# First expert layer: expert outputs scaled by their gates on leaving PSUM and summed by accumulating scatters in a chain; the tail reads one row per token

## The reference

```python
x = x + gnn0(layernorm(x))          # masked attention over a graph
x = x + ffn0(layernorm(x))          # experts, the two best of 8 for each token
x = x + gnn1(layernorm(x))          # message passing, two dense layers
x = x + ffn1(layernorm(x))          # attention, then the single best of 8 experts
```

```python
raw_weights = softmax(flat_x @ gate_w + gate_b)
top_w, top_idx = top_k(raw_weights, 2)
gate_output = (one_hot(top_idx, 8) * top_w[..., None]).sum(axis=-2)
h = gelu(einsum('td,edh->teh', flat_x, w1) + b1)
expert_out = einsum('teh,ehd->ted', h, w2) + b2
combined = einsum('ted,te->td', expert_out, gate_output)
```

## Time and profile before

| | us |
|---|---|
| median of 3 runs | 1104.51 (1102.79 to 1106.34) |
| the profiled execution | 1104.55 |
| its span, first to last instruction | 1102.8 |
| PE, DVE, ACT, POOL busy in the span | 884.4, 764.6, 506.7, 360.4 |
| first expert layer: first gather to the next normalisation | 345.06 to 467.49 |

### The profile page before, as it was taken

The page is one execution under the profiler, slowest core; times in us unless marked ns, Lnnn a source line. Parts: engine busy times, 40 slices in busy tenths (PEclk is TensorE's granted clock), DMA queues, the critical chain, the costliest instruction groups (busy, mean ns, idle before and its releaser), DMA issues.

```text
span 1102.8 us, 13781 instructions
## 1 busy us (share of the span) xinstructions
PE 884.4 (80%) x4522; PEld 675.1 (61%) x4522; DVE 764.6 (69%) x1545; ACT 506.7 (46%) x880; POOL 360.4 (33%) x238
## 2 busy tenths in 40 slices
PE   2999998878953999298898789999999888445990
PEld 2877773337742887077686567777777666334860
DVE  8879599886687443856122767787777776895638
ACT  3467527655362554132302146666665655542530
POOL 1000000000023453007330337786785766602520
PEclk9999999999985999589998999999999998966985
DMA  5010000013371444423110320020010230552442
GB/s 157 29 22 1 1 1 1 1 56 137 113 268 48 135 153 143 163 96 102 52 53 14 105 77 1 20 58 20 1 29 20 72 101 1 168 203 63 151 147 90
DMA packets 55523, 84.74 MB, mean 77 GB/s; under 512 B 8976, under 2 KB 31760, under 8 KB 54944
## 3 DMA queue, kind: packets, MB, share of 16 engines
q1 hardware_dynamic: 49376, 63.94, 18.3%
q0 software_dynamic: 6080, 19.93, 5.5%
HBM read 57.11 MB, written 22.54 MB: 72 GB/s over the span
## 4 chain that ended last, share of the span: by engine, by line
PE 57%; DVE 34%; ACT 4%; issue 3%; POOL 1%; DMA 1%; DVEq 0%; ACTq 0%; POOLq 0%
PE PS L324 37%; DVE late_columns L1133 4%; PE PS L1915 3%; PE PS L1930 3%; DVE neg_max L1488 3%; PE PS L1904 3%; DVE APL L971 2%; PE PS L1929 2%; DVE count_rows L1113 2%; PE PS L1823 2%; PE PS L1604 2%; PE PS L1766 2%; DVE early_columns L1133 1%; DVE XN L1004 1%; DVE stats L979 1%
## 5 line engine op out<-in xcount | busy, mean ns | idle before, releaser
L611 POOL TENSOR_SCALAR AP__193<-AP__193,rden 128x1024 f32<-128x1024 f32 x64 | 181.9, 2847 | 86.4 <-DVE rden L1493 85.7
L553 POOL TENSOR_TENSOR W1L<-W1R,W1H 128x1024 fp32r<-128x1024 f32 x9 | 21.0, 2362 | 307.3 <-ACT W1H L643 307.3
L643 ACT ACTIVATE APH<-PS 128x512 fp32r<-128x512 f32 x128 | 71.7, 597 | 70.1 <-PE PS L1915 45.7
L1488 DVE TENSOR_REDUCE neg_max<-PS 128x1 f32<-128x1024 f32 x64 | 78.2, 1222 | 36.9 <-PE PS L1904 36.0
L971 DVE TENSOR_TENSOR APL<-PS,APH 128x512 fp32r<-128x512 f32 x128 | 82.9, 679 | 23.8 <-ACT APH L643 23.5
L324 PE MATMUL PS<-XTH,WH 128*128 128x512 f32 x224 | 81.5, 411 | 4.5 <-DVE XTL L971 4.5
L1915 PE MATMUL PS<-ident,AP__193 128*128 128x128 f32 x512 | 71.2, 281 | 11.6 <-DVE APL L971 10.8
L324 PE MATMUL PS<-XTL,WH 128*128 128x512 f32 x224 | 78.1, 396 | 0.0
L324 PE MATMUL PS<-XTH,WL 128*128 128x512 f32 x224 | 77.8, 394 | 0.0
L1915 PEld LDWEIGHTS PS<-ident,AP__193 128*128 128x128 f32 x512 | 59.9, 144 | 28.3 <-issue 17.2
L914 ACT ACTIVATE AP__193<-PS,neg_max 128x1024 f32<-128x1024 f32 x64 | 71.5, 1117 | 7.3 <-DVE neg_max L1488 6.6
(11 more groups left out here) (297 smaller groups left out, 2423.4 us busy)
## 6 DMA issues: line engine op xcount, KB each, us to landing
YT<-expert_rows SPq DMA_DIRECT2D x12, 512.0 KB, 6.8
counts<-CT SPq DMA_DIRECT2D x8, 512.0 KB, 4.9
W1R<-in_L_ffn_w SPq DMA_DIRECT2D x8, 512.0 KB, 8.7
W2R<-in_L_ffn_w SPq DMA_DIRECT2D x8, 512.0 KB, 5.3
normalised<-XN SPq DMA_DIRECT2D x2, 2048.0 KB, 8.0
CG<-counts SPq DMA_DIRECT2D x8, 512.0 KB, 3.3
RAW<-in_L_gnn_W SPq DMA_DIRECT2D x16, 256.0 KB, 2.7
W1R<-in_L_ffn_W SPq DMA_DIRECT2D x8, 512.0 KB, 8.6
```

The lines of the kernel that those rows point to most:

```text
L611: gp.tensor_scalar(AP_[:, i % 4, :], AP_[:, i % 4, :], rden[:, i % 4:i % 4 + 1], None, ALU.mult).then_inc(B["norm"], 1)
L643: act.activation(dst, src, Copy, **kw).then_inc(s, 1)
L1488: v.tensor_reduce(out=neg_max[:, i % 4:i % 4 + 1], in_=banks(2 * (i % 2)), axis=X_AXIS, op=ALU.max, negate=True).then_inc(B["mx"], 1)
```

## The change

In the first expert layer the rows of a token are summed in DRAM, and each is scaled before.

- The rows that POOL gathers are 520 wide: 512 features and the token's eight gates (`xg_d`). SP stores the normalised rows into it as before, and the gates behind them when they are known (`gates_saved`). POOL's first gather waits for both. The buffers are six (`BXG`), in place of three.
- DVE copies the gate of the block's expert from the gathered row into `slot_gate`, one column of 128, ahead of the bias add. ACT's copy from PSUM to `BY` multiplies by it.
- Both choices of a token go to row `token` of `y_d`, by scatters with `compute_op=add`. So that two of them never touch a row together, each scatter waits until the one before has landed. The rows are cleared at the start of the kernel: POOL fills a tile `YZ` with zeros and SP stores it eight times over (2 MB, `y_clear`).
- The routing needs two DVE instructions fewer, since the row of a choice and the token are now the same; the picking of gates (`gate_of_choice`) goes.
- In the tail SP reads four times 512 KB, one row per token, straight after the last scatter, and loads the count tiles behind them. DVE adds plainly, with the statistics one tile behind. The two `diagonal` edits stand after the last add.

The second expert layer's work is unchanged, except that the semaphores' counts shift.

```diff
+    slot_gate = const("slot_gate", [P, 4], F32)
+    BXG = arena("BXG", [P, 6, WIDE], F32, 32)
+    YZ = arena("YZ", [P, D], F32, 64)
@@ sync
+        wait(setup, 14)
+        sp.dma_start(y_d[0:N, :].rearrange("(t p) d -> p t d", p=P), YZ[:, :].unsqueeze(1).to_broadcast([P, NT, D])).then_inc(y_clear, 16)
...
+            rows = xg_d[:, 0:D] if which == 0 else xn_d
+            sp.dma_start(rows.rearrange("(t p) d -> p t d", p=P), XN[:, :, :]).then_inc(M["xn_saved"], 16)
...
-                for c in range(CHOICES[which]):
-                    sp.dma_start(YT[:, c, 2 * g:2 * g + 2, :],
-                                 y_d[c * N + 2 * g * P:c * N + (2 * g + 2) * P, :].rearrange("(t p) d -> p t d", p=P)).then_inc(M["y_in"][g], 16)
+                sp.dma_start(YT[:, 0, 2 * g:2 * g + 2, :],
+                             y_d[2 * g * P:(2 * g + 2) * P, :].rearrange("(t p) d -> p t d", p=P)).then_inc(M["y_in"][g], 16)
...
+        wait(M["gates"], 1)
+            sp.dma_start(xg_d[:, D:WIDE].rearrange("(t p) e -> p t e", p=P), gates[:, :, :]).then_inc(gates_saved, 16)
         wait(A["stored"], 16 * NT)
-        wait(M["y_ps"], BLOCKS[0])
+        results(0)
         gcount_in(0, 0)
         gcount_in(1, 1)
-        results(0)
@@ gpsimd
+        gp.memset(YZ[:, :], 0.0).then_inc(setup, 1)
...
+                if which == 0:
+                    if b >= 6:
+                        wait(M["h_b1"], b - 5)
+                    gp.indirect_dma_start(out=BXG[:, b % 6, :], out_offset=None, in_=xg_d[:, :],
+                                          in_offset=at).then_inc(M["rows_in"][b % 6], 16)
...
+            if which == 0:
+                wait(gates_saved, 16)
+                wait(y_clear, 16)
...
                 wait(M["y_sb"], g + 1)
+                if which == 0:
+                    if b:
+                        wait(M["rows_out"][(b - 1) % 2], 16 * ((b - 1) // 2) + 16)
+                    gp.indirect_dma_start(out=y_d[:, :], out_offset=to, in_=BY[:, g % 2, :], in_offset=None,
+                                          compute_op=ALU.add).then_inc(M["rows_out"][g % 2], 16)
@@ scalar
+            if i == 1:
+                act.wait_ge(y_clear, 16)
...
+                if which == 0:
+                    act.wait_ge(M["h_b1"], g + 1)
+                    copy(BY[:, g % 2, :], PS[:, 6 + g % 2, :], M["y_sb"], scale=slot_gate[:, b % 4:b % 4 + 1])
@@ vector
-                own(v.tensor_scalar(slot_f[:, 1, 0:nb], slot, float(N), float(N), ALU.is_gt, ALU.mult))
-                v.wait_ge(M["routed"], routed(which, "experts"))
-                step(v.tensor_scalar(expert_f[:, 0:nb], slot, -1.0, 0.0, ALU.add, ALU.max))
-                v.tensor_tensor(gather_i[:, 0:nb], expert_f[:, 0:nb], slot_f[:, 1, 0:nb], ALU.subtract).then_inc(M["routed"], 1)
+            v.tensor_scalar(gather_i[:, 0:nb], slot, -1.0, 0.0, ALU.add, ALU.max).then_inc(M["routed"], 1)
...
+                if which == 0:
+                    if b >= 4:
+                        v.wait_ge(M["y_sb"], b - 3)
+                    v.tensor_copy(slot_gate[:, b % 4:b % 4 + 1], BXG[:, b % 6, D:WIDE][:, ds(e)])
...
+            for t in range(NT + 2):
+                if t < NT:
+                    add_rows(t)
+                if 0 <= t - 1 < NT:
+                    v.bn_stats(stats[:, t - 1, :], acc[:, t - 1, :]).then_inc(LN["dve"], 1)
+                if t >= 2:
+                    v.bn_aggr(mv[:, k, :], stats[:, k, :]).then_inc(LN["dve"], 1)
+                if which == 0 and t == NT:
+                    diagonal(0)
+                    diagonal(1)
```

More of the change, by code:

```diff
@@ L46, in build @@
     CHOICES = (2, 1)
-    STEPS = (37, 22)
+    STEPS = (29, 22)
+    WIDE = D + NEXP
     POOL_LO = (3, 6)
@@ L251, in build @@
     xn_d = nc.dram_tensor("normalised", (N, D), F32, kind="Internal").ap()
-    y_d = nc.dram_tensor("expert_rows", (CHOICES[0] * N + BLOCKS[0] * P, D), F32, kind="Internal").ap()
+    xg_d = nc.dram_tensor("normalised_gates", (N, WIDE), F32, kind="Internal").ap()
+    y_d = nc.dram_tensor("expert_rows", (N + BLOCKS[0] * P, D), F32, kind="Internal").ap()
     x_d = nc.dram_tensor("x_saved", (P, NT * D), F32, kind="Internal").ap()
@@ L287, in build @@
                          "xn_saved added x_ps x_hi x_lo h_ps h_b1 gelu t_ps t_hi t_lo y_ps y_sb w_lo_dve",
-                         w_in=2, rows_in=3, rows_out=2, y_in=4)
+                         w_in=2, rows_in=6, rows_out=2, y_in=4)
+    y_clear, gates_saved = sem("y_clear"), sem("gates_saved")
     def routed(which, what):
@@ L419, in _ @@
         load_w2(0, a["L0_ffn_w2"], 6, NEXP)
+        wait(M["gates"], 1)
+        with nc.allow_non_contiguous_dma(reason="eight gates behind each row"):
+            sp.dma_start(xg_d[:, D:WIDE].rearrange("(t p) e -> p t e", p=P), gates[:, :, :]).then_inc(gates_saved, 16)
         wait(A["stored"], 16 * NT)
-        wait(M["y_ps"], BLOCKS[0])
+        results(0)
         gcount_in(0, 0)
         gcount_in(1, 1)
-        results(0)
         wait(Q0["bias"], 1)
@@ L518, in _ @@
         gp.memset(neg_col[:, :], NEG).then_inc(setup, 1)
-        wait(setup, 10)
+        gp.memset(YZ[:, :], 0.0).then_inc(setup, 1)
+        wait(setup, 11)
         gp.affine_select(out=ident[:, :], in_=ident[:, :], compare_op=ALU.not_equal, fill=1.0,
@@ L559, in gather @@
             def gather(b):
[L560 to L565, removed]
+                at = bass.IndirectOffsetOnAxis(ap=gather_i[:, b:b + 1], axis=0)
+                if which == 0:
[3 more added lines that the diff above has]
+                                          in_offset=at).then_inc(M["rows_in"][b % 6], 16)
+                    return
+                if b >= 3:
+                    wait(M["x_ps"], first + b - 2)
+                gp.indirect_dma_start(out=BX[:, b % 3, :], out_offset=None, in_=xn_d[:, :],
+                                      in_offset=at).then_inc(M["rows_in"][b % 3], 16)
             wait(M["routed"], routed(which, "scatter"))
             wait(M["xn_saved"], 16 * which + 16)
+            if which == 0:
+                wait(gates_saved, 16)
+                wait(y_clear, 16)
             for b in range(5):
@@ L575, in expert_rows @@
                 wait(M["y_sb"], g + 1)
-                gp.indirect_dma_start(
-                    out=y_d[:, :], out_offset=bass.IndirectOffsetOnAxis(ap=scatter_i[:, b:b + 1], axis=0),
-                    in_=BY[:, g % 2, :], in_offset=None).then_inc(M["rows_out"][g % 2], 16)
+                to = bass.IndirectOffsetOnAxis(ap=scatter_i[:, b:b + 1], axis=0)
+                if which == 0:
[3 more added lines that the diff above has]
+                                          compute_op=ALU.add).then_inc(M["rows_out"][g % 2], 16)
+                else:
+                    gp.indirect_dma_start(out=y_d[:, :], out_offset=to, in_=BY[:, g % 2, :],
+                                          in_offset=None).then_inc(M["rows_out"][g % 2], 16)
         expert_lo(0)
@@ L835, in out_rows @@
                 act.wait_ge(M["y_ps"], g + 1)
-                copy(BY[:, g % 2, :], PS[:, 6 + g % 2, :], M["y_sb"])
+                if which == 0:
+                    act.wait_ge(M["h_b1"], g + 1)
+                    copy(BY[:, g % 2, :], PS[:, 6 + g % 2, :], M["y_sb"], scale=slot_gate[:, b % 4:b % 4 + 1])
+                else:
+                    copy(BY[:, g % 2, :], PS[:, 6 + g % 2, :], M["y_sb"])
             rows_hi(0)
@@ L1023, in _ @@
         v.wait_ge(edges_in, 32)
-        v.wait_ge(setup, 13)
+        v.wait_ge(setup, 14)
         per_tile = [P, NT, EC]
@@ L1343, in moe @@
             v.wait_ge(M["gates"], which + 1)
[L1345 to L1348, removed]
             for b in range(nb):
@@ L1357, in moe @@
                     v.tensor_tensor(X[:, b - 2, :], X[:, b - 2, :], row0[:, :], ALU.add).then_inc(F["beta"], 1)
-                if which == 0 and 2 <= b < 4:
-                    gate_of_choice(b - 2)
             assert steps[0] == STEPS[0] + which * STEPS[1], steps
@@ L1365, in moe, with add_rows @@
             v.wait_ge(M["acc"], which * NT + NT)
[L1366 to L1396, removed]
+            stats_before = (2, 5)[which] * (2 * NT + 4)
+            def add_rows(t):
+                v.wait_ge(M["y_in"][t // 2], 16 * which + 16)
+                v.tensor_tensor(acc[:, t, :], acc[:, t, :], YT[:, 0, t, :], ALU.add).then_inc(M["added"], 1)
+            for t in range(NT + 2):
+                if t < NT:
+                    add_rows(t)
+                if 0 <= t - 1 < NT:
+                    v.wait_ge(M["added"], NT * which + t)
+                    v.bn_stats(stats[:, t - 1, :], acc[:, t - 1, :]).then_inc(LN["dve"], 1)
+                if t >= 2:
+                    k = t - 2
+                    v.wait_ge(LN["dve"], stats_before + max(2 * k + (k + 1 < NT), 1))
                     v.bn_aggr(mv[:, k, :], stats[:, k, :]).then_inc(LN["dve"], 1)
+                if which == 0 and t == NT:
+                    diagonal(0)
+                    diagonal(1)
```

(11 more changed lines are left out.)

10 lines of the change are left out of this document (2 added, 8 removed).

## The result

| | us |
|---|---|
| before, median | 1105.42 (1102.79 to 1110.54) |
| after, median of 6 runs | 1147.93 (1147.44 to 1154.20) |
| ratio | 1.0383, 95% interval 1.0360 to 1.0406 |
| profiled execution after, its span | 1147.54, 1145.8 |

The change makes the kernel 3.8% slower. The direction was forecast, the size was not: 1122 us, range 1101 to 1141.

A forecast was written before the change was run, and what follows sets the result against it. TensorE was taken to bound the loop at 3.48 us a block, the scatter chain to replace it at 4.5. Normalisation 17.3 later, start +0.45, routing −0.3: +17.5 on 1104.55 gives 1122 us, range 1101 to 1141.

The forecast's parts named there:

- What decides: First expert layer's loop: only something longer than TensorE's 3.48 us a block costs time; the chained scatters decide.
- The break-even of 3.67 us: Time between successive scatter landings at which the change costs nothing; each further tenth of a microsecond costs 2.1 us.
- L = 3.4 + 0.8 + 0.3 = 4.5: Loop: microseconds between successive scatter landings, as plain scatter with start, plus second DRAM read, plus later start of that read.
- the rival in series: Loop: a whole gather, then a whole scatter, 5.9 us between landings, perhaps more POOL descriptors; 1153 us, chance 0.12.
- later start: Adding scatter in the loop: a read from DRAM starts 0.3 us later than one from SBUF.
- The base of 3.4: Loop: plain scatter, 3.13 us from issue to the waiting read, plus 0.28 for POOL to start after release.
- The clock: Loop: TensorE's granted clock, 1.00 before, was not expected to fall from idling; a fall would slow everything further.
- Only the second read: Loop: old rows requested together with new ones, so 3.4 + 0.8 = 4.2 us between landings; 1116 us, chance 0.24.
- The two hidden rivals: Loop stays TensorE-bound: 1102 us, chance 0.20; with ACT's table also loaded in time, 1099 us, chance 0.08.
- Start: Kernel start: POOL's zero fill delays DVE's first instruction by 0.45 us; the 2 MB clear costs nothing.
- Routing: Before the loop: two fewer DVE instructions bring the first gather 0.3 us earlier; waiting for stored gates costs nothing.
- Tail: Layer's end: adds and statistics 10.4 us, diagonals 0.6; ACT's late table load gives back 2.7 us before normalisation.

The follow-up runs named there:

- the plain chain: Changed kernel whose scatters still wait for each other but no longer add, keeping only a token's last choice: 1105.2 us, ratio 0.9990.
- the half rows: Changed kernel whose scatters add only 256 of 512 features, which the tail reads twice: 1131.59 us, ratio 1.0209.
- The half-row pairs: Changed kernel with 256 of 512 features scattered, adding (1131.59 us) and not adding (1100.68 us), each beside its whole-row counterpart (1147.93 and 1105.2 us).
- both repairs: Changed kernel, POOL's wait for the previous scatter put first, diagonals between sixth and seventh adds: 1138.88 us; with scatters also not adding, 1099.87 us.

## Why the prediction was right in its direction and wrong in its size

*What decides.* Right. The loop's limit moved from TensorE to the chain of scatters. The break-even of 3.67 us wasn't tested closely: the plain chain at 3.5 showed no measurable change and the half rows at 4.65 a loss of 2%, and no run lies between.

*The step that failed: "L = 3.4 + 0.8 + 0.3 = 4.5".* The accumulation was mis-sized: its landing took 4.8 us against 2.8 for a plain one, 2.0 more instead of 1.1. Of it, 0.6 is POOL's longer instruction; I had it at nothing, though the rival in series named it. The other 1.4 is behind POOL, where I had 0.8 + 0.3: the half-row pairs put about 1.0 of it down to the bytes and leave about 0.4, each give or take 0.2. So the bytes and the rest were a little too cheap, and most of what I missed is POOL's 0.6. That the rest is a "later start" isn't shown. The share of the queue has the second read too cheap as well: 8.0% of 1145.8 us over 16 engines, less 0.80 for each of the 53 plain transfers, is 2.1 us for each of the 23 accumulating scatters, over 2.5 times as much, where I had twice.

The base of 3.4 held (3.5 in the plain chain) by luck, since two errors cancelled. The landing was 2.8 instead of 3.13: the earlier trace rows was one scatter, and the same one takes 2.83 in after up to SP's read (1108.48 to 1111.31). And the next start took 0.77 instead of 0.28: I gave POOL one wait and left out the second and its order. With the waits exchanged it is 0.27, as forecast, and L = 5.17. So the error of 1.08 in L is 0.9 from the accumulation and 0.5 from the start, less 0.3 from the landing; over the chain it makes 21 × 1.08 = 22.7 us.

*The clock.* I wrote that I didn't expect a lower one. In the loop it fell to 0.92 at little cost, since TensorE waited anyway; but the `b2` products, behind an idle stretch of 5.52 us, ran at 0.50 throughout and took 14.02 instead of 10.97: 3.0 us, on the path. Before, the first of them still ran at 1.00. Then 1122 + 22.7 + 3.0 = 1147.7, against 1147.54 of the profiled execution; what is left over in the small terms cancels. The same sum fits the run with the waits exchanged, where the products took 14.02 us too: 390.3 + 21 × 5.17 + 3.0 = 501.9 for the normalisation, and it starts at 502.19.

*The rivals.* Neither account of the add was right. "Only the second read" would land after 3.13 + 0.8 = 3.9, "in series" after about 5.6; it was 4.8, and the 0.77 to the next start made it 5.58. The Trainium skill, Collectives: The Full Stack, section "The bandwidth ceiling: the fold count and why AG ≠ RS ≠ AR", halves the rate for two source reads, in ring collectives. The half-row pairs put some 1.0 of the 1.4 us behind POOL down to the bytes, and their two to three times doesn't rule a factor of 2 out; whether two reads are the reason no run shows. The kernel lost far more than the 1116 us worked out from it, since POOL's part and the order of waits come on top. The two hidden rivals gave 1102 and 1099 for an accumulation that is free: 1105.2 (1102.71 in the profiled execution) and 1099.87, there with both repairs, were measured. The first fits by its total only: it has the products end at 449.56 and the normalisation start at 464.6, and in the plain chain that was 453.01 and 467.84.

*Start.* DVE's first instruction at 4.49 instead of 4.02: +0.47, forecast +0.45. The clear held nobody back: it landed 9.2 us after its issue at 10.44, and the copy that waits for it ran at 40.83. *Routing.* The first gather starts at 344.09 instead of 345.06, −0.97 where start and routing summed to +0.15; about 0.7 of this had come back before 311 us, in work that the change doesn't touch. It bought nothing: the first scatter starts at 362.68, 0.7 later than before. TensorE's granted clock was 0.60 instead of 0.69 between 345 and 362 us, which is the likely reason. The gates were stored at 333.98 and never held the gather.

*Tail.* Adds, statistics and diagonals took 10.76 us (forecast 11.0), the root started 2.96 after the variances (2.9), the normalisation 4.04 after them (4.0). The path that I laid behind the last `BY` copy, with the rows read in its shadow, held, but for the clock.

## What to carry to other kernels

A scatter that must wait for the one before is priced by its whole latency, of which the bytes are only a part: compare issue to landing, plus the start of the next, with the time that the bound engine takes for a block. Here a plain transfer fitted by accident to a tenth of a microsecond, and the add broke it by two. If sums must meet in DRAM, transfers with rows of their own can overlap, which took the loss away here but gained nothing over the kernel before. And when a stage is slowed, ask at which clock the engine that now idles will do its next piece of work.

## What the runs showed of the hardware

- POOL's part of an accumulating scatter is longer by 0.6 us and doesn't shrink with the bytes: 1.59 us instead of 0.99, for rows of 2 KB and of 1 KB alike. The queue has 64 packets more for each, and as many for 1 KB as for 2 KB.
- An accumulating scatter of 128 rows of 2 KB landed 4.8 us after its issue, a plain one 2.8; with rows of 1 KB it was 3.9 and 2.4.
- POOL started a scatter 0.77 us after the landing with the wait for `BY` ahead of the one for the landing, and 0.27 us after it with the two exchanged, although the wait for `BY` had long been met in both.
- The `b2` products took 14.02 us at a granted clock of 0.50. Before, with a mean of 0.72 over the 16 us from 434, they took 10.97.
